# Attentions with their projections ahead of the rounds, squares ahead of weighted copies, probabilities turned by VectorE in blocks

## The reference

```python
x = x + L0_attn(layernorm(x))     # 16 heads of 8; low-rank q and kv, rope part and plain part added
x = x + L0_ffn(layernorm(x))      # six layers, each: local attention and a gated feed-forward
x = x + L1_attn(layernorm(x))     # 16 heads of 8, rope, full softmax over 512 keys
x = x + L1_ffn(layernorm(x))      # 16 experts, top-1 routing, capacity 160

# one layer of L0_ffn; shift moves the upper 64 features one token down
q, k, v = split(shift(x) @ Wqkv)              # 16 heads of 64
q = rotary(l2norm(q) * qs); k = rotary(l2norm(k) * ks)
sim = 8 * q @ k.T                             # windows of 32 queries, 64 keys, masked
x = softmax(sim) @ v @ Wo + x
xn = layernorm(shift(x)) * g + b
a, gate = split(xn @ W1 + b1)
x = (a * gelu(gate)) @ W2 + b2 + x
```

## Time and profile before

| | |
|---|---|
| median of 3 runs | 3033.61 us (3021.97 to 3043.45) |
| the profiled execution | 3019.82 us |
| its span, first to last instruction | 3018.0 us |
| PE busy | 2409.4 us (80%) |
| DVE busy | 1761.8 us (58%) |
| ACT busy | 1646.0 us (55%) |
| POOL busy | 1425.8 us (47%) |
| mean granted TensorE clock | 0.917 |

### The profile page before, as it was taken

One profiled execution on the slowest core, in us unless ns is written; L12 is line 12 of the kernel. 1 busy time (PEld: TensorE's weight loads), 2 busy tenths in 40 slices (PEclk: granted clock), 3 DMA queues, 4 the chain that ended last, 5 costly groups with the idle time before them and its releaser, 6 DMA issues.

```text
span 3018.0 us, 57906 instructions
## 1 busy us (share of the span) xinstructions
PE 2409.4 (80%) x23892; PEld 1401.5 (46%) x23892; DVE 1761.8 (58%) x1991; ACT 1646.0 (55%) x1955; POOL 1425.8 (47%) x1031
## 2 busy tenths in 40 slices
PE   5777768898888888888989988898889867777353
PEld 1111225665555555566656555565556511122253
DVE  1655647866666675667666776676677327673101
ACT  2144656766656666666666666666666411556100
POOL 2222027766655665566555666666556231210202
PEclk9988989999999999999999999999999856999677
DMA  4111000000000000000000000000000011110122
GB/s 149 53 39 42 14 1 16 2 2 16 1 24 2 15 2 2 24 2 15 2 24 2 16 2 9 17 15 2 1 9 1 1 45 46 47 47 15 39 70 65
DMA packets 62500, 67.48 MB, mean 22 GB/s; under 512 B 13142, under 2 KB 51156, under 8 KB 62228
## 3 DMA queue, kind: packets, MB, share of 16 engines
q1 hardware_dynamic: 60100, 58.90, 6.4%
q0 software_dynamic: 2128, 4.72, 0.6%
HBM read 45.91 MB, written 17.56 MB: 21 GB/s over the span
## 4 chain that ended last, share of the span: by engine, by line
PE 56%; ACT 17%; issue 12%; DVE 10%; POOL 2%; DMA 1%; SPq 0%; ACTq 0%; DVEq 0%; POOLq 0%
PE bank L849 10%; PE bank L931 7%; DVE big L1429 5%; PE bank L892 4%; PE bank L923 4%; PE bank L716 3%; PE bank L687 3%; PE bank L901 3%; ACT pxs L1288 3%; PE bank L669 3%; ACT big L1168 2%; ACT big L1253 2%; PE bank L968 2%; PE bank L974 2%; ACT L1310 2%
## 5 line engine op out<-in xcount | busy, mean ns | idle before, releaser
L591 POOL TENSOR_TENSOR sc<-sc,small 128x1024 f32<-128x1024 f32 x96 | 263.5, 2745 | 491.7 <-DVE small L1564 491.7
L1429 DVE TENSOR_REDUCE big<-bank 128x1 f32<-128x512 f32 x512 | 325.5, 685 | 203.7 <-PE bank L687 197.1
L1522 DVE TENSOR_REDUCE small<-big 128x32 f32<-128x2048 f32 x96 | 219.5, 2286 | 267.6 <-ACT big L1253 267.6
L931 PE MATMUL bank<-pxs,mw 128*128 128x256 f32 x1536 | 365.0, 381 | 0.0
L849 PE MATMUL bank<-wqk,xs 128*128 128x512 f32 x768 | 356.3, 607 | 8.8 <-ACT xs L1240 8.3
L931 PEld LDWEIGHTS bank<-pxs,mw 128*128 128x128 f32 x1536 | 289.5, 191 | 99.5 <-issue 69.0
L1288 ACT ACTIVATE pxs<-bank 128x1024 f32<-128x1024 f32 x192 | 186.2, 1022 | 166.1 <-PE bank L923 159.0
L1168 ACT ACTIVATE big<-bank 128x1024 f32<-128x1024 f32 x256 | 248.5, 1026 | 41.5 <-PE bank L701 41.0
L1528 DVE TENSOR_TENSOR big<-big,rotCl 128x2048 f32<-128x2048 f32 x96 | 222.9, 2322 | 30.0 <-POOL big L570 30.0
L1543 DVE TENSOR_TENSOR big<-big,small 128x1024 f32<-128x1024 f32 x192 | 239.7, 1249 | 1.1 <-POOL small L581 1.1
L569 POOL TENSOR_TENSOR big<-big,rotSl 128x1024 f32<-128x1024 f32 x96 | 227.2, 2367 | 8.9 <-ACT big L1245 8.7
(11 more groups left out here) (214 smaller groups left out, 4263.6 us busy)
## 6 DMA issues: line engine op xcount, KB each, us to landing
pxs<-part_rows SPq DMA_DIRECT2D x64, 224.0 KB
part_rows<-big SPq DMA_DIRECT2D x96, 128.0 KB
wqk<-in_L_ffn_w SPq DMA_DIRECT2D x32, 256.0 KB, 3.1
wqk<-in_L_ffn_Wqkv SPq DMA_DIRECT2D x12, 512.0 KB, 4.4
wvt<-in_wv_layers_t SPq DMA_DIRECT2D x6, 512.0 KB, 5.2
wol<-in_L_ffn_Wo SPq DMA_DIRECT2D x6, 512.0 KB, 6.9
w<-in_L_ffn_W SPq DMA_DIRECT2D x6, 341.0 KB
pxs<-big SPq DMA_DIRECT2D x96, 4.0 KB
```

Of the source, the lines that this page charges most:

```text
L591: pool.tensor_tensor(p3, p3, rden(i).unsqueeze(2).broadcast_to([P, LH, 64]), ALU.mult).then_inc(l_pn, 1)
L931: m = pe.matmul(bank[:, 6, part * 2 * P:(part + 1) * 2 * P], mw[:, 2 * (a % 4) + s, a // 4, :], pxs[:, part, a, s, :], start=(a == 0 and s ...
L1429: dve.tensor_reduce(nm[:, qt, 2 * p + r:2 * p + r + 1], bank[:, 4 + r, :], AX.X, ALU.max, negate=True).then_inc(a_mx, 1)
```

## The change

Three parts.

**Attentions.** Four projections are in flight, through banks 0 to 3; the means use bank 6, the variances bank 7. Centred inputs, squares and raw projections have two buffers each (`xc_of`, `sq_of`, `raw_of`, `parts_of`), and the values go into `zT`. All projections stand ahead of round 0: sequences 0 and 1 first (both means and variances before the first projection), then 3 and 2 (`ORDER`) among the maxima of sequence 0 (`first_maxima`). The rounds keep maxima, scores, weighting and finish, with maxima and scores taking turns one by one. Each part goes to DRAM once (3 writes for q, 3 for k), to a place for each sequence, and is read as often as needed: 12 loads for a half stack in place of 4. The maxima rows' ones are loaded straight into the stack. SP writes the parts of 3 and 2 before it moves the maxima of 0.

**ACT's order in a layer.** `squares(T+2)` stands ahead of `weighed`, right after the takes.

**Probabilities.** DVE transposes `probs` in its 32x32 blocks, between `square_sums` and `turn_plain`; PE's `turn_probs` and ACT's `turned_probs` are gone. A block puts 32 keys of one head and window on 32 partitions, so `weigh` is 8 matmuls of 32x128 by 32x512 in four row groups, two accumulating steps for each of four banks (4, 5, 2, 3), and both copies can start only near its end. The inputs come as two plain transposes of 128 tokens (`xnat`) in place of eight matmuls. The projection of keys waits for `keys` instead of `turned_probs`, since banks 0 and 1 no longer take probabilities.

```diff
 # layers, PE
-            def turn_probs(T, i):
-                pe.wait_ge(l_pn, T + 1)
-                for c in range(PAIRS):
-                    t = pe.transpose(bank[:, c // 4, (c % 4) * P:(c % 4 + 1) * P], probs(i)[:, c * P:(c + 1) * P], ident[:, :])
-                t.then_inc(l_pt, 1)
...
+                for half in range(2):
+                    s = i * P + half * WIN
+                    t = pe.transpose(bank[:, 4, half * P:(half + 1) * P], xs[:, b % 2, s:s + P], ident[:, :])
+                t.then_inc(l_xt, 1)
+
+            def weigh(T, i):
+
+                p4 = sc[:, 2, :].rearrange("p (h v t) -> p h v t", h=LH, v=2)
+                for half in range(2):
+                    for w in range(4):
+                        m = pe.matmul(bank[:, (4, 5, 2, 3)[w], :], xnat[32 * w:32 * w + 32, i % 2, half, :],
+                                      p4[32 * w:32 * w + 32, :, half, :], start=(half == 0), stop=(half == 1),
+                                      tile_position=(32 * w, 0), skip_group_check=True)
+                        if half == 1 and w % 2 == 1:
+                            m.then_inc(l_px, 1)
...
 # layers, slot on PE
-                    pe.wait_ge(l_pe, T)
+                    pe.wait_ge(l_pt, T)
                     pe.wait_ge(l_e, T + 1)
-                    weigh(T - 1, i + 3, 0)
                     if ahead >= 2:
                         pe.wait_ge(l_raw, 2 * T + 5)
...
-                    weigh(T - 1, i + 3, 1)
+                    weigh(T - 1, i + 3)
...
 # layers, slot on ACT
-                if not (first and i == 0):
-                    turned_probs(T - 1)
                 exponentials(T, i)
                 if ahead >= 2:
                     take(T + 2, i % 2, 0)
                     take(T + 2, i % 2, 1)
...
+                if ahead >= 2:
+                    squares(T + 2, i % 2)
                 if not (first and i == 0):
                     for half in range(2):
                         weighed(T - 1, it if i else it - 1, (i - 1) % TILES, half)
-                if ahead >= 2:
-                    squares(T + 2, i % 2)
                 windows(T, i)
...
 # layers, DVE
+            def turn_probs(T, i):
+                if not (isinstance(T, int) and T == 0):
+                    dve.wait_ge(l_px, 2 * T)
+                dve.wait_ge(l_pn, T + 1)
+                settle(dve)
+                dve.transpose(sc[:, 2, :], probs(i)).then_inc(l_pt, 1)
...
                 if ahead >= 1:
                     square_sums(T + 1, (i + 1) % 2)
+                if not (first and i == 0):
+                    turn_probs(T - 1, (i - 1) % 2)
+                if ahead >= 1:
                     turn_plain(T + 1, (i + 1) % TILES)
                     add_queries(T + 1, (i + 1) % 2)
...
 # attentions, PE
+            def first_maxima(a):
+
+                for u in range(UNITS):
+                    for s in range(4 * u, 4 * u + 4):
+                        maximum(a, 0, s)
+                        if s == 0:
+                            mean_in(a, 3)
+                        if s == 4:
+                            variance_in(a, 3)
+                        if s >= 12 and s % 2 == 0 and (s - 12) // 2 < NEV[a]:
+                            project_in(a, 3, (s - 12) // 2)
+                        if s == 31:
+                            mean_in(a, 2)
+                        if s == 35:
+                            variance_in(a, 2)
+                        if s == 41:
+                            pe.wait_ge(ln_r, (ATT1 if a else 0) + 4)
+                            turn_maxima(a, 0, 0)
+                        if s >= 43 and s % 2 == 1 and (s - 43) // 2 < NEV[a]:
+                            project_in(a, 2, (s - 43) // 2)
+
+            def round_of(a, b):
 
                 n = a * BATCH + b
...
+                for u in range(UNITS):
+                    for s in range(4):
+                        if b + 1 < BATCH:
+                            maximum(a, b + 1, 4 * u + s)
+                        if s < 2 and u + 1 < UNITS:
+                            scores_t(a, b, 2 * u + 2 + s)
+                        if s == 2:
+                            weigh_all(a, b, u)
...
             def attention(a):
                 pe.wait_ge(step_done, (ATT1 if a else 0) + 1)
                 for b in range(2):
...
+                    mean_in(a, b)
+                    variance_in(a, b)
+                for b in range(2):
+                    for e in range(NEV[a]):
+                        project_in(a, b, e)
+                first_maxima(a)
+                pe.wait_ge(a_raw[a], BATCH * NEV[a])
+                pe.wait_ge(a_one, 64 * (a + 1))
+                for b in range(BATCH):
+                    begin_round(a, b)
                     round_of(a, b)
...
 # attentions, SP
                 for b in range(2):
                     write_parts(a, b)
                     for half in range(2):
                         load_stacks(a, b, half)
+                for b in ORDER[2:]:
+                    write_parts(a, b)
                 for half in range(2):
                     move_maxima(a, 0, half)
...
+                for b in range(1, BATCH):
                     for half in range(2):
...
+                        move_maxima(a, b, half)
+                        if b + 1 < BATCH:
+                            load_stacks(a, b + 1, half)
```

## The result

The changed kernel takes 2910.39 us (median of 4 runs, 2895.91 to 2917.88) against 3030.38 us beside it. The ratio is 0.9597, 95% interval 0.9562 to 0.9633: 4% faster. I had forecast 2800 us with a range of 2725 to 2905. The direction was right; the gain was little more than half of what I summed, and the time lies just outside the range.

The account below looks back on a forecast made before the run. PE (88% busy) looked like the layers' bound, but not alone: ACT's chain and a POOL-DVE loop of 16.4 us also bound slots. 3018 - 140 (layers) - 86 (attentions) = 2792, 2794 with 1.8 outside the span; forecast 2800 us, range 2725 to 2905.

Parts of the forecast that it names:

- POOL's floor of 16.4 in the third interval: Layers: POOL's normalising and swapped multiplies, then DVE's multiply and add, 12.9 + 2.3 + 1.2 us, limit a slot.
- Rival (a): Layers: DVE's block transpose needs what POOL holds, or is slow; 86 us more, 2885 us; chance 0.2.
- Rival (b): Layers hardly gain: row groups overlap only in pairs, bank 4 wait in full, PE's halts stay; 2895 us; chance 0.13.
- wait for bank 4: Layers, PE: window transposes wait for the first weighted copy to clear the bank, about 1.0 us without a feed matmul between.
- Over the 96 reductions the four intervals are 23.6, 19.0, 18.3 and 19.6 in the mean: Layers: four score-to-score intervals, 80.5 us together, fall to 74.2; gain 6.3 x 22 = 139, taken as 140.
- 23.6 - 1.9: Layers, first interval: earlier squares and a smaller window copy shorten ACT's chain by 1.9 us, to 21.7.
- PE is full only in the second (18.69 of 18.69): Layers, four profiled slots: PE is busy throughout the second interval only, 18.69 us.
- DVE's sum of 17.8: Layers, second interval: DVE's operations after the change add up to 17.8 us, making DVE itself the bound.
- My allowance, 0.7 per four slots: Layers: PE's unexplained halts in score matmuls, left in at 0.7 us per four slots where slack doesn't take them.
- 138, against 133.6: First attention: round 0 starts at 138 us, after projections, POOL's rotations and SP's writes; 4.5 later than before.
- rival (c): First maxima run with PE slow, 2.1 us per projection; rounds start 20 later in each attention: 2840 us; chance 0.12.
- interleaving single maxima may save 0.1 us a step, so 56 each: Attentions: rounds 0 to 2 run like the old round 2, 56 us each with single maxima, bounds 50 and 60.

Follow-up runs that it names:

- without the small operation: Changed kernel without DVE's 32-element tensor_scalar behind the square sums, its factors moved into other operations' constants: 2883.93 us, 0.951.
- changing one order: Changed kernel with SP moving sequence 0's rows of maxima ahead of sequence 2's parts, in both attentions: 2874.63 us, 0.9462.
- the paired order: Changed kernel with PE's rounds back to two scores, a pair of maxima, two scores, a pair of maxima, weighing: 2924.32 us, 0.9626.

## Why the prediction was wrong

The change is faster, as forecast, but the gain is little more than half of the sum. In the profiled execution 102 us are missing against the sum (2792 and 2894): 23 ahead of the layers, 52 in them, 27 behind them.

**Right.** The block transpose (1.2 forecast, 1.231 measured) and its place; the weighing at 2.00; DVE's wait for squares gone; POOL's floor of 16.4 in the third interval (16.36); the first maximum (66 forecast, 63.65), as four banks let the projections run back to back. Rival (a) fell for the transpose: POOL does not lock it out. But its mechanism was real for other operations, and I had seen it only in the earlier trace rows. Rival (b)'s pairs did not come. Its wait for bank 4 did (mostly 0.7, 1.2 and 1.0 us in the first, third and fourth interval, none in the second). I read it as free, since ACT or POOL's floor held those intervals; no run prices it.

**The layers, step "Over the 96 reductions the four intervals are 23.6, 19.0, 18.3 and 19.6 in the mean".** From one set I took the gains and floors, and set them against the mean of all.
- First interval: 23.6 - 1.9. The 1.9 was mostly the 1.74 us that ACT idled ahead of the weighted copies in that set. It did so in the ten sets with b = 1 or 2 behind the first three; in those with b = 0 or 3 it idled 0 to 0.19, and ACT's chain was already without a gap:

```profile
756.08 1.94 ACT L1288 ACTIVATE pxs<-bank 128x1024 f32<-128x1024 f32 x2 [0.17 <-PE bank L923]
```

  There the squares gained nothing (23.93 to 24.00, 22.98 to 23.12); with b = 1 they gained 1.7. The mean gain was 0.55, not 1.9.
- Second: "PE is full only in the second (18.69 of 18.69)" was read as a bound and was none. What ends the interval is DVE's reduction of the scores, and in none of the 22 later sets did it wait for them, before or after: it starts 1.8 us behind PE's scores in the mean before, 2.7 after. In the earlier trace rows's set PE was through with the scores at 1542.55, and DVE was late from its wait for the squares on:

```profile
1541.07 1.48 PE L892 MATMUL bank<-kbuf,qT 64*32 64x64 f32 x128
```
```profile
1537.33 2.29 DVE L1522 TENSOR_REDUCE small<-big 128x32 f32<-128x2048 f32 x1 [1.26 <-ACT big L1253]
...
1543.89 1.21 DVE L1549 TENSOR_REDUCE small<-bank 128x16 f32<-128x1024 f32 x1
```

  With the squares alone moved, this interval is 17.41 us with PE busy 17.36 (17.4 to 17.9 in the others without tables): that was PE's own share, not 18.7. DVE's sum of 17.8 was near: the typical interval is 18.1, and without the small operation mostly 17.4 to 17.9. What I had left out are the next layer's tables, which DVE makes in this slot in b = 3 (sets of five layers). Before, their three operations took 1.8 us and lengthened the interval to 20.5 to 20.8. Now the last two stand beside POOL's sum of keys in all five sets and take 2.95 in place of 0.85, the lock again, and the interval is 22.0. These rows are the two operations before and after, and POOL's sum:

```profile
1376.51 0.85 DVE L1575 TENSOR_TENSOR rotSl<-rotS,qks 128x256 f32<-128x256 f32 x2
```
```profile
1295.12 2.95 DVE L1612 TENSOR_TENSOR rotSl<-rotS,qks 128x256 f32<-128x256 f32 x2
```
```profile
1295.27 2.52 POOL L593 TENSOR_TENSOR big<-big 128x1024 f32<-128x1024 f32 x1
```

  Gain 0.14, not 1.2.
- Third: 16.5 forecast, 16.54 measured. The floor of 16.4 holds for b = 1 and 2; that the mean fits too is luck, with 17.36 for b = 0 and 15.93 for b = 3.
- Fourth: 17.5. It is 17.5 and 17.3 for b = 2 and 3. For b = 0 the layer's mixed weights are made there (18.8). For b = 1 the loop over layers turns (19.9), and PE stands 3.93 us with nothing to wait for:

```profile
1170.11 1.97 PE L866 MATMUL bank<-ident,big 128*128 128x128 f32 x8 [3.93 <-issue]
```

  The kernel before had this halt too, 2.7 to 3.2 us in four sets. My allowance, 0.7 per four slots, counted only the halts in the score products. Gain 1.26, not 2.1.

Together 3.7 us a set of four for the 6.3 of the forecast; 2.6 a set is 57 us over 22 sets, for the 52 that are missing.

**The attentions, step "138, against 133.6".** Round 0 started at 142.5. The first maxima ended as forecast (122.9); POOL's rotations ended at 135.64, not 130, since they began at 115.82 where I had the fifth projection at 110; from there 6.8 us to the start, where I had 8. In the second attention the same steps gave a start 23 us later than before, counted from its first matmul, not 12: its first maxima took 62 us, not 58, and the pause behind them 12.5, where the forecast's own numbers leave 5. Its clock was 0.61 there, and the first projections among the maxima took 2.07 us each, which is rival (c) in part. The kernel before is no witness for a high clock here: its 1.00 of the earlier trace rows for the first maxima is not what PE ran at, since a pair of products took 0.61 us there, as in its second attention at a granted 0.50, and takes 0.39 in its round 2 at 1.00:

```profile
84.21 0.61 PE L687 MATMUL bank<-pxs 64*128 64x512 bf16 x2 [0.69 <-ACT kbuf L1151]
```

I had SP's wait in the sum and took it as given; changing one order took 36 us off.

**The attentions, step "interleaving single maxima may save 0.1 us a step, so 56 each".** Rounds took 57.7, 65.2, 61.1 and 56.5, 68.2, 64.5: 37 us more than six times 56. I had carried the clock of 1.00 of the old round 2 over to new products, though my own range of 50 to 60 had no term for it. With 64 rows 16 of the 37 come back. The other 21 lie in the four rounds with a tail, 61 where I had 56: 3 over the old round 2, and 2 that single maxima were to save and saved only in steps without the tail's transposes (3.09 in place of 3.30). Two steps at the start of round 0 run at the low clock behind the pause (the weighing 1.93 in place of 1.06).

## What to carry to other kernels

A floor read in one iteration holds for iterations like it. Tabulate the interval by its position in every loop it lies in before subtracting from a mean, and add what only some positions carry. An engine that is busy throughout an interval need not bound it: look at what the instruction that ends it waited for. Two edits that each open one of two loops of like length can be worth little alone and more together; price them as a pair. Where a queue serves a stage that is waiting, what it serves for a later stage goes behind, and an activation-table change that two operations can share is worth looking for first: it gave more here than the attentions' whole rework.

## What the runs showed of the hardware

- The granted clock of TensorE went with the rows its products worked in: in the paired order, rounds at 48 and 56 rows ran at 0.57 to 0.92, with 56 to 64 at 0.89 to 0.94, with 64 in both at 0.93 to 0.97. In the single order only 64 in both made a difference (six rounds 357.2 us against 367.8 to 380.6 in eleven traces). Rows of zeros seem to be enough (359.3). In the first maxima 64 rows changed nothing (0.74 against 0.73), so it isn't the rows alone; why they matter is open.
- A DVE block transpose of 128x1024 fp32 takes 1.23 us, beside a long POOL operation too (68 of 96); a 32-element tensor_scalar takes 0.18 to 2.02, long beside POOL's multiplies. DVE's multiply beside POOL's addition took 2.98 in place of 1.2, two table operations 2.95 in place of 0.85, and POOL's addition beside DVE's 3.38 in place of 2.35.
- A pause of 4.3 us on PE cost it twice: the gate matmul behind it took 2.00 in place of 1.09, and the scores 2.06 in place of 1.49, at a granted 0.50.
